# Graph-attention block: mask bytes turned in 32x32 squares by VectorE and DMA in place of TensorE transposes

## What is computed

```python
h = relu(layernorm(x))
Wh = h @ W
e = leaky_relu(Wh @ a1 + (Wh @ a2).T, 0.2)
att = softmax(where(adj > 0, e, -9e15), axis=-1)
x = x + relu(att @ Wh)
h = relu(layernorm(x))
node = h @ W1
msg = einsum("nk,nkf->nf", node, einsum("nc,kcf->nkf", h, W2))
x = x + relu(adj @ msg + node @ b)
```

## Time and profile before

| | |
|---|---|
| median of 3 runs | 1872.01 us (1871.8 to 1873.08) |
| the profiled execution's own time | 1872.76 us |
| its span, first to last instruction | 1871.2 us |
| granted TensorE clock, mean | 0.993 |
| TensorE busy | 1831.2 us, 98% |
| ScalarE, VectorE, POOL busy | 1330.3, 1209.9, 714.5 us |
| moved by DMA | 452.24 MB, mean 242 GB/s |

### The profile page before, as it was taken

One profiled execution on the slowest core, in us unless ns is written; L12 is line 12 of the kernel. 1 busy time (PEld: TensorE's weight loads), 2 busy tenths in 40 slices (PEclk: granted clock), 3 DMA queues, 4 the chain that ended last, 5 costly groups with the idle time before them and its releaser, 6 DMA issues.

```text
span 1871.2 us, 38399 instructions
## 1 busy us (share of the span) xinstructions
PE 1831.2 (98%) x13404; PEld 1590.1 (85%) x13404; DVE 1209.9 (65%) x1511; ACT 1330.3 (71%) x2144; POOL 714.5 (38%) x530
## 2 busy tenths in 40 slices
PE   7799999999999999999999999999999999999998
PEld 4699989889889888988988888898877788888886
DVE  6666677677767767777776776776656543443534
ACT  4666788877878787887788778878465655555554
POOL 0300056546546655654665564565535400000000
PEclk9899999999999999999999999999999999999999
DMA  9488967776776776777777677674753344445430
GB/s 332 154 311 320 352 243 283 289 276 265 287 288 251 295 290 251 288 284 274 271 287 278 263 292 280 251 295 156 309 198 144 141 161 161 154 159 205 152 157 22
DMA packets 105812, 452.24 MB, mean 242 GB/s; under 512 B 6736, under 2 KB 15136, under 8 KB 87968
## 3 DMA queue, kind: packets, MB, share of 16 engines
q1 hardware_dynamic: 86720, 356.53, 51.2%
q10 hardware_dynamic: 12208, 75.62, 9.9%
q0 software_dynamic: 6832, 19.41, 2.8%
HBM read 364.46 MB, written 87.07 MB: 241 GB/s over the span
## 4 chain that ended last, share of the span: by engine, by line
PE 91%; DVE 3%; ACT 2%; issue 2%; SPq 1%; DMA 1%; DVEq 0%; ACTq 0%
PE ot_ps L806 47%; PE mt_ps L850 13%; PE ot_ps L850 13%; PE hw_ps L770 11%; PE mt_ps L738 6%; ACT wh_mask L505 1%; PE h_ps L765 1%; DVE att L947 1%; DMA adj_sb<-in_adj_dram 1%; SPq L283 1%; DVE p_sb L971 1%; DVE p_sb L897 1%; ACT prod L571 1%; DVE keep L952 0%; PE h_ps L777 0%
## 5 line engine op out<-in xcount | busy, mean ns | idle before, releaser
L806 PE MATMUL ot_ps<-wh_mask,p_sb 128*128 (+1 forms) x8192 | 980.6, 277 | 5.8 <-DVE p_sb L971 5.8
L971 DVE SCALAR_TENSOR_TENSOR p_sb<-zb,qcol,mt 128x1024 f32<-128x1024 uint8 (+1 forms) x512 | 780.6, 1555 | 263.3 <-ACT mt L517 212.2
L806 PEld LDWEIGHTS ot_ps<-wh_mask,p_sb 128*128 128x128 f32 x8192 | 942.3, 192 | 7.7 <-issue 5.9
L378 POOL TENSOR_TENSOR prod<-prod 128x1024 f32<-128x1024 f32 (+2 forms) x192 | 408.0, 2125 | 516.5 <-ACT prod L571 500.6
L505 ACT ACTIVATE wh_mask<-adj_sb 128x2048 uint8<-128x2048 f32 x256 | 492.9, 1928 | 3.3 <-DMA adj_sb<-in_adj_dram 2.2
L632 ACT ACTIVATE mask<-adj_sb 128x1024 fp32r<-128x1024 uint8 x240 | 255.4, 1065 | 176.5 <-PE ot_ps L850 176.4
L517 ACT ACTIVATE mt<-mt_ps 128x1024 uint16<-128x1024 uint16 x256 | 267.5, 1046 | 151.8 <-PE mt_ps L738 150.5
L1009 DVE CAST mask<-adj_sb 128x1024 fp32r<-128x1024 uint8 x272 | 202.3, 750 | 248.5 <-PE mt_ps L850 246.6
L571 ACT ACTIVATE prod<-hw_ps,node 128x128 f32<-128x128 f32 x1024 | 278.8, 385 | 92.1 <-PE hw_ps L770 92.1
L850 PE MATMUL mt_ps<-mask,msgs 128*128 128x512 f32 x1024 | 283.0, 398 | 4.3 <-issue 3.4
L850 PE MATMUL ot_ps<-mask,msgs 128*128 128x512 f32 x1024 | 275.6, 391 | 0.8
(11 more groups left out here) (112 smaller groups left out, 612.5 us busy)
## 6 DMA issues: line engine op xcount, KB each, us to landing
adj_sb<-in_adj_dram SPq DMA_DIRECT2D x128, 2048.0 KB, 8.4
maskT_d<-mt ACTq DMA_DIRECT2D x64, 1024.0 KB, 5.2
adj_sb<-maskT_d SPq DMA_DIRECT2D x32, 2048.0 KB, 7.7
keep_d<-keep POOLq DMA_DIRECT2D x64, 128.0 KB, 6.0
p_sb<-keep_d SPq DMA_DIRECT2D x4, 2048.0 KB, 12.2
msg_d<-msg POOLq DMA_DIRECT2D x56, 128.0 KB, 5.9
msgs<-msg_d SPq DMA_DIRECT2D x7, 1024.0 KB, 10.2
wh_mask<-in_x_dram SPq DMA_DIRECT2D x8, 512.0 KB, 7.3
```

What stands on the lines that cost most here:

```text
L378: pool.tensor_tensor(prod[:, 0:n, :], prod[:, 0:n, :], prod[:, n:2 * n, :], ALU.add)\
L806: ins = pe.matmul(ot_ps[h][:, (t - t0) * ROW:(t - t0 + 1) * ROW], p_sb[:, r, t * P:(t + 1) * P], rows, start=False, stop=end and t == t1 - 1)
L971: dve.scalar_tensor_tensor(p_sb[:, r, :], zbf[:, bass.ds((ib % 2) * BLK, BLK)], qcol[:, bass.ds(tile + b_, 1)], mtb[:, p, k, :, b_], ALU.m ...
```

## The change

The turned mask no longer passes through TensorE and ScalarE. VectorE turns 32-bit words (four mask bytes each) within squares of 32 x 32, one instruction for a whole block, into a second part of `wh_mask` that was `m8`'s second buffer; `m8` is now single. SP stores the squares to `maskT_d` in four DMAs, one for each group of 32 partitions, so that they land at their turned places, waits until they have landed, and loads the turned block back into `mt` with one DMA. The numbering of rows becomes `i * 1024 + t * 128 + r * 4 + a` on partition `a * 32 + r` for the adjacency, which SP now loads in four DMAs of 32 partitions for each half, and `i * 1024 + y * 512 + p * 4 + b` for `x`, the residual and the output, each in two DMAs. A byte of a word is a row tile, so `weigh` and the conversions read bytes four apart instead of two. ScalarE's casts move to the first two chunks of a turn and wait for the squares of the turn before. The diff, cut to its core:

```diff
-    adj_v = adj.rearrange("(i p t) n -> i p t n", p=P, t=T)
-    x_v = x.rearrange("(i p t) f -> i p t f", p=P, t=T)
+    SQ = 32
+    A = P // SQ
+    Y = T // 4
+    adj_v = adj.rearrange("(i t r a) n -> i a r t n", t=T, r=SQ, a=A)
+    x_v = x.rearrange("(i y p b) f -> i y p b f", y=Y, p=P, b=4)
...
-    maskT_d = nc.dram_tensor("maskT_d", [NB, NB, P, C * BLK], U16).ap()
+    maskT_d = nc.dram_tensor("maskT_d", [NB, NB, Y, P, A, T * SQ], FP32).ap()
...
-        mt = sb("mt", [P, 2, C, BLK], U16)
+        mt = sb("mt", [P, 2, Y, BLK])
...
+        m8w = wh_mask[:, NT * (D + 2):NT * (D + 2) + BLK * T // 4].rearrange("p (t c s) -> p t c s", t=T, s=SQ)
+        sq = wh_mask[:, NT * (D + 2) + BLK * T // 4:].rearrange("p (c w) -> p c w", w=T * SQ)
+        sq_t = wh_mask[:, NT * (D + 2) + BLK * T // 4:].rearrange("p (c t r) -> p t c r", t=T, r=SQ)
...
+            def turn_back(i, ib, jg, p):
+                n = 2 * i + p
+                block = maskT_d[bass.ds(2 * jg + p, 1), bass.ds(ib, 1), :, :, :, :]
+                sp.wait_ge(squared, n + 1)
+                sp.sem_inc(past_sp, 1)
+                for a in range(A):
+                    sp.dma_start(block[:, :, :, :, a, :].rearrange("j i y (x s) w -> (j i s) (y x) w", s=SQ),
+                                 sq[a * SQ:(a + 1) * SQ, :, :]).then_inc(sq_stored, 16)
+                sp.wait_ge(sq_stored, 16 * A * (n + 1))
+                sp.sem_inc(past_sp, 1)
+                sp.wait_ge(p_ready, READY + T * (n - 1))
+                sp.sem_inc(past_sp, 1)
+                sp.dma_start(mt[:, p, :, :], block.rearrange("j i y p a w -> (j i p) y (a w)")).then_inc(mt_in[p], 16)
 
             def turn(i, ib, jg, finish, last):
                 for p in range(2):
                     for h in range(2):
                         q = 2 * p + h
                         sp.wait_ge(adj_cast[q], i)
-                        sp.dma_start(adj_sb[:, q, :].rearrange("p (t n) -> p t n", n=BLK),
-                                     adj_v[bass.ds(ib, 1), :, h * HT:(h + 1) * HT,
-                                           bass.ds((2 * jg + p) * BLK, BLK)].rearrange("i p t n -> (i p) t n"))\
-                          .then_inc(adj_in[q], 16)
+                        for a in range(A):
+                            sp.dma_start(adj_sb[a * SQ:(a + 1) * SQ, q, :].rearrange("r (t n) -> r t n", n=BLK),
+                                         adj_v[bass.ds(ib, 1), a, :, h * HT:(h + 1) * HT,
+                                               bass.ds((2 * jg + p) * BLK, BLK)].rearrange("i r t n -> (i r) t n"))\
+                              .then_inc(adj_in[q], 16)
+                    if not isinstance(jg, int) or jg > 0:
+                        turn_back(i - 1, ib, jg - 1, p)
+                    elif not (isinstance(ib, int) and ib == 0):
+                        turn_back(i - 1, ib - 1, IT - 1, p)
...
+            for p in range(2):
+                turn_back(NB * IT - 1, NB - 1, IT - 1, p)
...
-            def cast(q, part, count, turned_before):
-
-                act.wait_ge(adj_in[q], 16 * count)
-                act.wait_ge(turned, turned_before)
+            def cast(q, part, count):
+
+                act.wait_ge(adj_in[q], 16 * A * count)
+                if part == 0 and q % 2 == 0 and not (q == 0 and isinstance(count, int) and count == 1):
+                    act.wait_ge(squared, 2 * (count - 1) + q // 2)
...
-            def evict(chunk, k, p, use):
...
-            def turn_mask(chunk, k, p, casts):
...
+            def turn_squares(n, p, count):
+                for h in range(2):
+                    dve.wait_ge(adj_cast[2 * p + h], count)
+                if not (isinstance(n, int) and n == 0):
+                    dve.wait_ge(sq_stored, 16 * A * n)
+                dve.transpose(sq_t, m8w).then_inc(squared, 1)
...
-                                         qcol[:, bass.ds(tile + b_, 1)], mtb[:, p, k, :, b_],
+                                         qcol[:, bass.ds(tile + b_, 1)], mtb[:, p, b_, :, k],
...
-                        dve.wait_ge(evicted, c + 1)
+                        if k == 0 and not (last and p == 1):
+                            turn_squares(n + 1, 1 - p, i + 1 + p)
+                        if k == 0:
+                            dve.wait_ge(mt_in[p], 16 * (i + 1))
...
-                        dve.tensor_copy(mask32[:, r, ib, :], masks[:, s % 4, ib, t % T // 2, :, t % 2])\
+                        dve.tensor_copy(mask32[:, r, ib, :], masks[:, s % 4, ib, t % Y, :, t % T // Y])\
```

More of the change, by code:

```diff
@@ L331, in _ @@
                 load_masks(0, s)
-            sp.wait_ge(turned, C * NB * NB)
-            for p in range(2):
-                sp.wait_ge(mt_stored[p], 16 * NB * IT)
             for r in range(4):
@@ L437, in _ @@
                 pool.wait_ge(p_used[r], 4 * NB * IT)
-            for p in range(2):
-                pool.wait_ge(mt_stored[p], 16 * NB * IT)
-            pool.wait_ge(turned, C * NB * NB)
+            pool.wait_ge(sq_stored, 16 * A * NB * NB)
             for mi in range(T):
@@ L480, in _ @@
             act.wait_ge(consts, 7)
[L482 removed]
+            act.sem_inc(out_stored, 32 * Y)
             def deviation(i):
@@ L509, in cast @@
                     ins.then_inc(adj_cast[q], 1)
-            def evict(chunk, k, p, use):
-                act.wait_ge(turned, chunk + 1)
-                if k == 0 and not (isinstance(use, int) and use == 0):
-                    act.wait_ge(p_ready, T * (2 * use + p - 1))
-                    act.wait_ge(mt_stored[p], 16 * use)
-                act.activation(mt[:, p, k, :], mt_ps[k % 2][:, :].bitcast(U16), ACT.Copy).then_inc(evicted, 1)
-            ahead = [(q, part) for q in range(4) for part in range(2 if q < 3 else 1)]
             deviation(0)
@@ L524, in _ @@
                 project(i)
-                if i:
-                    cast(*ahead[i - 1], 1, 0)
-            evict(0, 0, 0, 0)
-            evict(1, 1, 0, 0)
+                if 1 <= i <= 4:
+                    cast((i - 1) // 2, (i - 1) % 2, 1)
+            for q in (2, 3):
+                for part in range(2):
+                    cast(q, part, 1)
             act.wait_ge(setup_dve, 13)
@@ L576, in load_xt @@
                 act.wait_ge(mv_done, T * pb + 1)
-                act.dma_start(xt[:, :, :], x_v[bass.ds(pb, 1)].rearrange("i p t f -> (i p) t f")).then_inc(xt_in, 16)
+                for y in range(Y):
+                    act.dma_start(xt[:, y:T:Y, :], x_v[bass.ds(pb, 1), y].rearrange("i p b f -> (i p) b f")).then_inc(xt_in, 16)
             def copy_sums(ib):
@@ L608, in turn @@
                             copy_sums(ib)
[L609 removed]
+                        if k < 2 and not last:
+                            for part in range(2):
+                                cast(2 * p + k, part, i + 2)
                         if finish:
                             u = i - IT
[L612 to L621 removed]
+                            finish_tile(k, p, u, 2 * u + p, 2 * jg + p, ib - 1)
             attention_loop(act, turn)
@@ L642, in store_out @@
                 act.wait_ge(out_ready, 4 * ii + 2 * h + 6)
[L643 to L644 removed]
+                for y in range(Y):
+                    act.dma_start(out_v[bass.ds(2 * ii + h, 1), y].rearrange("i p b f -> (i p) b f"),
+                                  outs[:, h * T + y:(h + 1) * T:Y, :]).then_inc(out_stored, 16)
             for t in range(2):
@@ L728, in _ @@
                     idle_run(8)
-            def turn_mask(chunk, k, p, casts):
-                if k == 0:
-                    for h in range(2):
-                        pe.wait_ge(adj_cast[2 * p + h], casts)
-                if not (isinstance(chunk, int) and chunk < 2):
-                    pe.wait_ge(evicted, chunk - 1)
-                words = mt_ps[k % 2][:, :].bitcast(BF16)
-                for t in range(T):
-                    ins = pe.transpose(words[:, t * P:(t + 1) * P],
-                                       m8[:, p, t, :].bitcast(BF16)[:, k:BLK // 2:C], ident16[:, :])
-                ins.then_inc(turned, 1)
             pe.wait_ge(hT_done, 2 * NB)
-            turn_mask(0, 0, 0, 1)
-            turn_mask(1, 1, 0, 1)
             pe.wait_ge(setup_dve, 4)
```

88 lines of the change are left out of this document (29 added, 59 removed).

## The result

The changed kernel takes 2385.74 us (median of 4 runs, 2382.53 to 2387.88) where the kernel before takes 1872.16 (4 runs beside it): a ratio of 1.274, interval 1.2719 to 1.2763. The profiled execution took 2382.53 us with a span of 2380.9.

What follows compares the result with a forecast made beforehand. TensorE bounds the kernel before; after the change SP's queue does, 20.5 + 5.1 + 2.6 + 2.6 = 30.8 us a turn. 61 such periods after the first mask at 91.8 us, plus the ending, give 2554 us, range 1960 to 2710.

Steps and rivals of the forecast that it cites:

- TensorE's gain: Attention loop: without mask transposes TensorE saves 1.64 us a turn, about 105 us if nothing else ends last.
- 11.9 us of work leave room for it: 0: ScalarE, per turn: losing four evictions leaves 11.9 us of work, so its casts' new wait for squares costs nothing.
- full rate: Rival: the narrow adjacency loads overlap and keep 410 GB/s, so the kernel takes 1800 us; chance 0.17.
- the ring: SP's queue: adjacency, squares out, landing wait and mask back pass in series each turn, 30.8 us together.
- Term 1, adjacency: SP's queue: loading 4.19 MB by 32 partitions a DMA at 205 GB/s takes 20.5 us a turn.
- Term 2, squares out: SP's queue: storing 1.05 MB of squares by 32 partitions at 205 GB/s takes 5.1 us a turn.
- Terms 3 and 4: SP's queue: 2.6 us empty while squares land, fitting other queues' 0.33 MB, then 2.6 us loading the mask back.
- the half rate: Likeliest case, chance 0.67: 230 to 187 GB/s, 28 to 33.2 us a turn, 2375 to 2710 us.
- the wait on squares: Profile sign: this wait, not that on the mask, as the largest idle time would show the forecast wrong.
- TensorE's clock: Attention loop: TensorE's 12 us waits may lower its clock, up to 4 us more a turn, still under 30.8.
- a quarter: Rival: each narrow load moves only its 32 partitions' share, 56.6 us a turn, 4195 us; chance 0.03.
- in between: Rival: the four narrow transfers partly overlap at 230 to 325 GB/s, 28 to 21.3 us a turn; chance 0.13.

Runs made afterwards that it cites:

- the last kernel: Changed kernel with rows renumbered for 128-partition loads, squares stored between halves, casts in ScalarE's gaps, x from two queues, output from SP: 1818.07 us, 0.9706 of the kernel before.
- the wide kernel: The changed kernel with each half-block loaded in four DMAs over all 128 partitions instead of 32, on permuted rows: 1901.63 us.
- The run on two queues: The changed kernel with loads for partitions 0 to 63 on SP's queue and 64 to 127 on ScalarE's: 2237.32 us.

## Why the prediction was right, and where its terms were off

*TensorE's gain and what bounds.* Right. TensorE's transposes are gone, and the last kernel shows what they were worth: 19.0 us a turn with finish steps for the 18.5 forecast. In block 0 it takes 17.7 for 14.7, at a DMA share of 1.00. In the changed kernel that gain lies off the path.

*VectorE, ScalarE.* The transpose is 2.31 us for 2.6, the byte step costs nothing (median weigh 1.281 us for 1.285), ScalarE has room. All held for the changed kernel. But "11.9 us of work leave room for it: 0" counted busy time; with wide loads ScalarE's waits for TensorE, in series with that work, were the limit of the turns with finish steps. The forecast for full rate, 1800 us, would have missed by 100: the wide kernel took 1901.63, with the ring not alone at fault: it sets the 20.0 us of block 0, the casts' place the rest.

*Term 1, adjacency.* 20.5 us forecast as a geometric middle, 19.3 measured (4.19 MB at 217 GB/s). The step itself, loads by 32 partitions at about half the rate, is right and carries the forecast. That the number came so near is in part luck: a middle of 102 and 410 GB/s is no mechanism, and no row pointed to half. The Trainium skill's estimate, 19.2 by "SBUF — State Buffer", "Door 1: The DMA port swizzle", agrees with the trace better than mine. The same page of the Trainium skill, section "Can I just issue two DMAs to hit both halves?", says that two concurrent DMAs on different halves gain only 6% over one. The run on two queues does not agree, with 346 and 332 GB/s where both were in flight and 208 from one, and the measurement decides.

*Term 2, squares out.* The term that was mis-sized. "The slower limit counts: 205 GB/s, 5.1 us" carried the loads' half rate over to stores. The windows show 376 to 383 GB/s for the four stores out of 32 partitions each: 2.8 us. The bound by run length alone, 3.0, was the right one.

*Terms 3 and 4.* About 2.5 us, by the shares of the four microseconds from 845 (0.44, 0.00, 0.43, 0.78), and 2.6: the four terms make 27.2 us. Hiding term 3 gave back 1.3 us. That the other queues' 0.33 MB fit into it was wrong; they move beside the adjacency. With 0.8 us for them the sum is 28.0, but in block 0, which has no such stores, a turn is 28.6 us all the same, so the account is not complete.

*Sum.* 30.8 us a turn forecast, 28.0 found, counted as the sum counts them, from the first weigh (90.0 us; 91.8 forecast) to the first one behind mask 61:

```profile
1798.70 1.46 DVE L957 SCALAR_TENSOR_TENSOR p_sb<-zb,qcol,mt 128x1024 f32<-128x1024 f32 x1 [3.28 <-DMA mt<-maskT_d]
```

61 x 2.8 = 171 us were too much, and that is the whole miss of the profiled execution (2554 forecast, 2382.53 found): the last three turns took 58.8 us to the last attention matmul at 1857.5 us, for 58.5 forecast, and what lies behind it kept its 523 us. The 27.7 between transposes has the short last turns in it. The time, 2385.74, lies in the half rate's own range, 2375 to 2710, near its fast end.

*The signs.* The one that I called wrong, the wait on squares as VectorE's largest, came true (465 us against 309 for the mask) without the ring being wrong: the transpose stands ahead of the weigh and waits for the store in the same ring. Wide loads, not the name of a wait, told the theories apart. TensorE's clock fell as expected, 0.80 in block 0: the same 8192 matmuls are busy for 1089.7 us, 967.1 in the last kernel, inside of the ring's wait.

*The rivals.* Full rate and a quarter are out: the loads move 217 GB/s. The border to "in between" was drawn at 230 GB/s over loads and stores; 5.24 MB in 19.3 + 2.8 us are 237, just past it, because the stores do not move at half rate. So the case that was named likeliest holds for the loads, and the whole sits on its edge. A quarter was seen, but from another cause, the four-step DMAs.

## What to carry to other kernels

Price a layout change by what it does to the DMAs' shape: how many partitions one load spans, and how many values its outermost step has. A slower transfer that just fits under the bounding engine, and a round trip that just fits, cost 52 and 30 us alone (the second with TensorE's gain taken off), and 514 in series on one queue. When an engine's work is moved, its waits between the steps count with its busy time; fill them, and see that what a single buffer's next writer waits for is done before the reader's turn begins.

## What the runs showed of the hardware that I had not expected

- Loads into 32 partitions move at 217 GB/s with the queue full; four stores out of 32 partitions each, one behind the other, at 376 to 383.
- Two such loads into different halves of the partitions, from two queues, move 332 and 346 GB/s together in two stretches in which both are in flight; one of them alone moves 208 in the same run.
- Stores on another queue move beside narrow loads: 286 GB/s together, at a share of 1.03.
- A load whose DRAM side has four outer steps keeps a full queue at a share of 0.26 and 104 GB/s.
- VectorE's transpose of 2048 words takes 2.31 us in unbroken runs and 3.91 us with words 32 bytes apart; ScalarE's cast to bytes 1.91 us, and 2.53 us with bytes four apart.
